# Layer 1's first two weights loaded during the feed-forward before it, and its preparations queued two blocks at a time

## The reference

```python
x = x + 0.5 * L0_ffn(layernorm(x))     # ternary weights, 8-bit activations, conv over time, silu
x = x + L0_attn(layernorm(x))          # softmax attention, 16 heads, bias b_o
x = x + 0.5 * L0_ffn(layernorm(x))
x = x + 0.5 * L1_ffn(layernorm(x))     # layer 1
x = x + L1_attn(layernorm(x))          # causal linear attention, strictly below the diagonal
x = x + 0.5 * L1_ffn(layernorm(x))
# L1_ffn:
p = softmax(x @ gate_W.T)                       # 8 experts
cnt[n, e] = number of experts of token n with p > 0.3, as a one-hot count
final = einsum over experts of (x @ expert_W[e].T) * cnt * p
return final @ out_W.T
```

## Time and profile before

| what | us |
|---|---|
| median of three runs | 3529.73 |
| the three runs | 3400.16, 3529.73, 3662.04 |
| the profiled execution | 3381.05 |
| span of its slowest core (3), first to last instruction | 3379.4 |
| spans of the other cores | 3299.0 to 3374.5 |
| TensorE busy, of the span | 2719.5 (80%) |
| VectorE busy | 1984.2 (59%) |
| ScalarE busy | 1703.0 (50%) |

### The profile page before, as it was taken

One profiled execution on the slowest core, in us unless ns is written; L12 is line 12 of the kernel. 1 busy time (PEld: TensorE's weight loads), 2 busy tenths in 40 slices (PEclk: granted clock), 3 DMA queues, 4 the chain that ended last, 5 costly groups with the idle time before them and its releaser, 6 DMA issues.

```text
span 3379.4 us, 39052 instructions; the slowest of 8 cores (3299.0 to 3379.4 us)
## 1 busy us (share of the span) xinstructions
PE 2719.5 (80%) x11770; PEld 1162.0 (34%) x11770; DVE 1984.2 (59%) x2842; ACT 1703.0 (50%) x2015; POOL 382.7 (11%) x437
## 2 busy tenths in 40 slices
PE   1355768799489999999999883678879959889789
PEld 0122223344133444444433331333334424334334
DVE  1477667775557777777765124677777514443433
ACT  2776656563423666666654623666656313414430
POOL 0000102112310001110000100001211211211310
PEclk7676889899798999999965796889989979999999
DMA  7343533233612022220110154122323360000001
GB/s 228 111 122 121 173 123 125 87 96 103 149 19 45 22 39 57 42 39 19 30 35 7 38 148 142 35 83 86 123 83 92 103 212 1 1 20 31 1 7 69
DMA packets 153945, 259.11 MB, mean 77 GB/s; under 512 B 37968, under 2 KB 74064, under 8 KB 153424
## 3 DMA queue, kind: packets, MB, share of 16 engines
q1 hardware_dynamic: 121312, 199.77, 19.4%
q0 software_dynamic: 32432, 56.83, 7.0%
HBM read 220.70 MB, written 52.56 MB: 81 GB/s over the span
## 4 chain that ended last, share of the span: by engine, by line
PE 61%; DVE 14%; ACT 9%; issue 8%; DMA 7%; POOL 1%; SPq 1%; DVEq 0%; ACTq 0%; POOLq 0%
PE fb L1099 11%; PE fb L869 8%; PE aups L1556 8%; PE apps L1670 7%; PE asps L1651 7%; PE mb L2169 6%; PE ajps L1520 3%; DVE fbig L910 2%; PE rs L2060 2%; DVE amx L1567 2%; ACT fbig L905 2%; PE mb L2224 2%; PE mb L1968 1%; DMA xbd<-alnb 1%; DMA fbig<-w1h 1%
## 5 line engine op out<-in xcount | busy, mean ns | idle before, releaser
L1567 DVE TENSOR_REDUCE amx<-aups 128x1 f32<-128x512 f32 x1024 | 662.6, 686 | 253.8 <-PE aups L1556 251.9
L1660 ACT ACTIVATE aet<-asps 128x1024 bf16<-128x1024 f32 x512 | 521.6, 1025 | 294.0 <-PE asps L1651 290.3
L869 PE MATMUL fb<-fxsc,fw1r 128*128 128x512 bf16 x2048 | 561.1, 415 | 96.4 <-DVE fbig L914 66.1
L1099 PE MATMUL fb<-fbig 128*128 128x512 bf16 x2048 | 504.1, 396 | 95.5 <-DVE fbig L839 53.8
L1556 PE MATMUL aups<-ahd 65*128 65x512 bf16 x1024 | 381.0, 415 | 22.1 <-DVE amx L1567 8.5
L1670 PE MATMUL apps<-aet,avt 128*65 128x512 bf16 x1024 | 339.8, 416 | 16.4 <-ACT aet L1660 11.0
L869 PEld LDWEIGHTS fb<-fxsc,fw1r 128*128 128x128 fp8e4 x2048 | 213.3, 105 | 400.6 <-issue 209.3
L1651 PE MATMUL asps<-ahd 65*128 65x512 bf16 x1024 | 340.0, 417 | 0.0
L1099 PEld LDWEIGHTS fb<-fbig 128*128 128x128 fp8e4 x2048 | 204.8, 101 | 362.2 <-issue 143.1
L910 DVE SCALAR_TENSOR_TENSOR fbig<-fb,cw2sb,fbig 128x511 f32<-128x511 f32 x256 | 191.3, 747 | 213.0 <-ACT fbig L905 210.8
L905 ACT ACTIVATE fbig<-fb,cbsb,cw2sb 128x512 f32<-128x512 f32 x256 | 196.3, 770 | 234.4 <-PE fb L869 222.0
(11 more groups left out here) (249 smaller groups left out, 2968.7 us busy)
## 6 DMA issues: line engine op xcount, KB each, us to landing
fw1r<-wq SPq DMA_DIRECT2D x224, 128.0 KB, 2.1
fbig<-wq SPq DMA_DIRECT2D x112, 256.0 KB, 2.7
fbig<-w1h SPq DMA_DIRECT2D x32, 512.0 KB, 12.9
fw2f<-w2h SPq DMA_DIRECT2D x64, 256.0 KB, 3.1
fbig<-w2h SPq DMA_DIRECT2D x28, 512.0 KB, 3.9
fxq<-x SPq DMA_DIRECT2D x8, 1024.0 KB, 9.0
fbig<-x POOLq DMA_DIRECT2D x32, 256.0 KB, 5.6
xa<-fbig POOLq DMA_DIRECT2D x32, 256.0 KB, 3.7
```

Source lines behind the costliest of these rows:

```text
L869: tp = T(lambda e, dc=dc: e.matmul(bank[b][:, :], sl[:, o + dc * 128:o + (dc + 1) * 128], xr[:, dc * 512:(dc + 1) * 512], start=(dc == 0), ...
L1099: tp = T(lambda e, j=j: e.matmul(bank[2 + j][:, :], w2r[s][:, o + j * 128:o + (j + 1) * 128], xi2[:, hc * 512:(hc + 1) * 512], start=(hc = ...
L1567: lambda e, hh=hh, c=c: e.tensor_reduce(m[:, c:c + 1], ups[hh][:, :], axis=AX.X, op=ALU.max),
L1660: ta = A(lambda e: e.activation(et[g % 3][:, :], sps[s][:, :], AF.Exp, scale=0.125), wait=[tp, tk.get(("ef", g % 3))])
```

## The change

Three shared places are made for the whole program: `sh_a` (16 KB a partition) serves as `xq` of the feed-forward, as `lnb` of the attention and as `qk` (so also `ow`) of layer 1; `sh_b` as `xsc`, `big2` and `xs[0]` (so also `e0`); `gw_sb` holds the gate weight, which is now loaded in the chain of constants at the head. `early_l1`, called at q = 4 of the second feed-forward, issues the loads of `owb` and `e0b` from SyncE as soon as the places are free, and `layer1` no longer issues them. In `center` POOL's subtraction of block k + 2 is emitted after the work on block k, and both preparations yield after the multiplications of blocks 1, 3 and 5, so that these go out in four pieces of two blocks. The function `attn_l0` is also moved up in the file, unchanged but for the two places.

```diff
+        gw_sb = sb("lgw", [128, DC * NE], F32)
+        sh_a = sb("sha", [128, DC * QT], F32)
+        sh_b = sb("shb", [128, 2 * DC * QT], BF16)
+        s_early = {k: em.sem("Se" + k) for k in ("ow", "e0")}
         s_pre = em.sem("Spre")
-        DMA_SEMS.append(s_pre)
+        DMA_SEMS += [s_pre] + list(s_early.values())
         pre = {}
...
         dma(CHX, cb_sb[:, :], cb_in.ap())
+        dma(CHX, gw_sb[:, :].rearrange("p (a m) -> p a m", a=DC),
+            gwT.ap().rearrange("(a p) m -> p a m", p=128))
         const_tag = dma(CHX, bo_sb[:, :], bo_in.ap())
...
                 em.wait_only(e, guard())
+        early = {}
+        def early_l1(w_a, w_b):
+            for key, dst, src, w in (("ow", sh_a[:, :].bitcast(BF16), owb,
+                                      w_a),
+                                     ("e0", sh_b[:, :], e0b, w_b)):
+                early[key] = em.go(
+                    "sync", lambda e, dst=dst, src=src: e.dma_start(
+                        dst.rearrange("p (a b) -> p a b", a=DC),
+                        src.ap().rearrange("(a p) m -> p a m", p=128)),
+                    wait=[pre[src.name]] + list(w), dma=s_early[key])
...
                 big = fsb("fbig", [128, 32 * 1024], F32)
-                xq = fsb("fxq", [128, DC * QT], F32)
+                xq = sh_a
                 xsb = fsb("fxs", [128, 2048], BF16)
...
                 xi8 = fsb("fxi8", [128, 2048], I8)
-                xsc = [fsb("fxsc", [128, DC * QT], BF16) for _ in range(2)]
+                xsc = [sh_b[:, i * DC * QT:(i + 1) * DC * QT]
+                       for i in range(2)]
                 acc = fsb("facc", [128, 1024], F32)
...
                     gen = first and q == 1
+                    if q == NQ and not first:
+                        early_l1([ln["xqfree"]], ln["xscfree"])
                     if q == 1:
...
                 wo = lsb("lwo", [128, KVC * D], BF16)
-                xs = [lsb("lxs", [128, 2 * DC * QT], BF16) for _ in range(2)]
+                xs = [sh_b, lsb("lxs", [128, 2 * DC * QT], BF16)]
                 xln = lsb("lxln", [128, DC * QT], BF16)
                 cb = [lsb("lc", [128, 512], F32) for _ in range(3)]
-                qk = lsb("lqk", [128, 4 * KVC * QT], BF16)
+                qk = sh_a[:, :].bitcast(BF16)
                 S_sb = lsb("ls", [128, KVC * KV], F32)
...
                 gt_sb = lsb("lgt", [8, 512], F32)
-                gw = lsb("lgw", [128, DC * NE], F32)
+                gw = gw_sb
                 gtok = lsb("lgk", [128, 128], F32)
...
                 s_o = dsem("lo")
-                s_g = dsem("lg")
...
-                tk["gw"] = dget(s_g, v3(gw[:, :], DC), gwT.ap().rearrange(
-                    "(a p) m -> p a m", p=128))
+                tk["ow"], tk["e0"] = early["ow"], early["e0"]
                 x_load(0)
-                w_load("ow", s_w[0], ow[:, :], owb, DC)
-                w_load("e0", s_w[1], xs[0][:, :], e0b, DC)
                 w_load("e1", s_w[2], xs[1][:, :], e1b, DC)
...
                         start=(dc == 0), stop=(dc == DC - 1)),
-                        wait=[tk["gw"]])
+                        wait=())
                 t = A(lambda e: e.mul(gtok[:, 0:NE], rs[0][:, 0:NE],
...
                 def center(q):
                     out = []
-                    for k in range(DC):
+                    def sub(k):
                         src = xq[q % 3][:, k * 512:(k + 1) * 512]
-                        t = G(lambda e, k=k, src=src: e.tensor_tensor(
+                        out.append(G(lambda e: e.tensor_tensor(
                             cb[k % 3][:, :], src, m_sb[:, :], ALU.subtract),
                             wait=[tk["m"], tk.get(("cf", k % 3)),
-                                  tk["x", q, k]])
-                        out.append(t)
-                        yield k, t
-                    tk["mf"] = t
+                                  tk["x", q, k]]))
+                    for k in range(2):
+                        sub(k)
+                    for k in range(DC):
+                        yield k, out[k]
+                        if k + 2 < DC:
+                            sub(k + 2)
+                    tk["mf"] = out[-1]
...
                         tk["cf", k % 3] = t
+                        if k % 2 == 1 and k < 7:
+                            yield
                     tk["rsf"] = [t]
...
                         tk["cf", k % 3] = t
+                        if k % 2 == 1 and k < 7:
+                            yield
                     tk["rsf"] = [t]
...
-                big2 = asb("abig2", [128, 4 * T], BF16)
+                big2 = sh_b
...
-                lnb = asb("alnb", [128, 4096], F32)
+                lnb = sh_a
```

947 lines of the change are left out of this document (472 added, 475 removed).

## The result

| | before | after |
|---|---|---|
| median of the runs of this comparison, us | 3464.94 (3394.69 to 3662.04) | 3489.99 (3348.45 to 3592.08) |
| ratio after / before, comparable runs | | 0.9863, 95% interval 0.9834 to 0.9891 |
| span of core 3 | 3379.4 | 3342.4 |
| core 3, layer 1 (start of the column means to the end of TensorE's last product) | 645.2 | 605.7 |
| core 3, TensorE busy | 2719.5 | 2715.6 |

In this comparison the changed kernel is about 1.4% faster, some 46 us of 3395. The medians say the opposite, because in some executions, the profiled one of the changed kernel among them, the cores of one die run at a lower clock and take up to 8% longer; the ratio leaves such executions out. Two later comparisons of the same two kernels gave 0.9883 (0.9841 to 0.9926) and 0.9915 (0.9893 to 0.9936), so about 1% is what all three bear out.

A forecast was written before the change was run, and what follows sets the result against it. TensorE's idle time in layer 1 was taken as the bound: the `e0b` wait and VectorE evictions. -16.2 - 0.9 + 2.6 - 23.8 = -38.3 us, off the median 3529.7 gives 3491; range 3339 to 3558.

The forecast's parts named there:

- The wait for `e0b`: Start of layer 1: TensorE's stand until `e0b` lands goes, so the fusion starts right after the column means, -16.2 us.
- second, third and fourth attention: Layer 1: preparations in pieces let evictions and output blocks come earlier, -3.8, -5.6 and -6.8 us.
- How the numbers follow: Closing step: 2% taken as tellable, sum taken off the median; faster 0.08, same 0.89, slower 0.03.
- Part 1, the two loads, w2's cover: Last feed-forward pass: early loads take 13.1 us, the w2 load queued behind keeps 6 us of cover, cost 0.
- Rival 4: Last feed-forward pass: the 4.19 MB hold back w2 loads; 14 us of wait at 112 GB/s; chance 0.04.
- The warmer clock: Start of the fusion: means running straight into it shorten its time at half clock, -0.9 us (0 to 1.75).
- The gate weight: Program's head: one more link in the chain of constants, +2.6 us; sign, first x load 2.4 to 3.9 later.
- The first attention: Layer 1: transposes end 5.1 us earlier, but the next normalisation's statistics slip three steps; -2.8 us.
- Rival 1: Layer 1 attentions: the statistics' slip takes the preparations' gain back to about 8 us, sum -22; chance 0.25.
- Rival 2: Layer 1: VectorE's order was the whole of the idle time, sum up to -78, middle -60 us; chance 0.13.
- Rival 3: Fusion start: early loads bring nothing because ScalarE's x casts delay TensorE; sum -21 us; chance 0.08.
- two signs that the prediction named for being wrong: Layer 1: TensorE waits longer for line 2350's evictions, or y blocks wait over 2 us a round for ScalarE's squares.

The follow-up runs named there:

- the preparations alone: Kernel before the change with only the two yields and the new `center`, weights still loaded in layer 1; ratio 0.9952 (0.9928 to 0.9976).
- the loads alone: Changed kernel with preparations in one piece and the old `center`; shared places, early loads and gate weight at the head kept; ratio 0.9973 (0.9948 to 0.9997).
- the last experiment: Changed kernel with statistics emitted beside the pieces, early loads behind the last w2 load, gate weight in layer 1; ratio to before 0.9843 (0.9827 to 0.986).

## Where the prediction was right, and the step that failed

**The sum.** -38.3 against -37.0 on the profiled core. The wait for `e0b`, the two normalisation places, second, third and fourth attention came within 0.3 us each. For the third attention some of that is luck: with the preparations alone the clock moved its length by over 2 us from core to core (76.1 against 73.5 to 73.7). That TensorE does not wait for the gate load in its 5 us behind SyncE's first issue held on core 3: 5.10 without the load, and 5.23 on seven cores when it was put back. It did not hold on every core: on core 6 of the kernel before it was the load that ended the wait, at 7.29. Three comparisons of the whole program (0.9863, 0.9883, 0.9915) lie around the forecast ratio of 0.9887.

**How the numbers follow** is the step that failed. "2% is about what a measurement of this kernel can tell from no change" stands there without a working; what it had at hand was the spread of three raw runs, 3400 to 3662. The runs showed a finer measure in its place: the ratio told 0.3% (0.9834 to 0.9891, and 0.2% to 0.4% in the repeats), and no change is outside all three intervals. A forecast of -1.1% should have been put as faster by a clear margin; the chance of 0.89 for no change, and 0.08 for faster, came from that one sentence. The second failing in the same paragraph is the base. Taking the sum off the median (3529.7) instead of off the profiled execution (3381.1 - 38.3 = 3343; the comparable runs of the changed kernel lay between 3338 and 3359) put the predicted time at 3491, a figure that depends on which of three widely spread runs is the middle one. The median of the changed kernel's four runs, 3490, fell next to it by chance; it is above the median of the kernel before, 3465, though the kernel is faster.

**Part 1, the two loads, w2's cover: wrong in size.** Forecast: issued at 2643, 13.1 us for both, first w2 load in by 2661, cover 6 us, cost 0. Measured: issued 2645.7 (SyncE was still issuing w2 loads to 2645.6), `e0b` landed 23.7 us later, at 2669.9, and the w2 product wanted at 2670.4 waited 0.37 us on core 3, 1.5 on core 2 and 3.9 on core 6. The w2 load that it waited for was issued at 2660.2 and took 10.4 us to land; in the kernel before the same load was issued at 2658.3, not 2656.5, and took 2.5. The term that was mis-sized is the rate: 321 GB/s was that of a stretch in which SyncE's queue moved 8.32 of the 8.34 MB. Here the engines moved

```profile
DMA packets 3323, 7.41 MB, mean 274 GB/s; under 512 B 224, under 2 KB 224, under 8 KB 3321
```

from 2645 to 2672, and only 4.19 of the 7.41 MB were the two weights; the rest were w2 weights, stores and residuals. Rival 4 named the place and the mechanism; its price was 0 to 4 us, and not 14 or more. The prediction cited the Trainium skill, "DMA: Bandwidth & Descriptors", Queues, rings and completion order, for the rule that a DMA engine consumes one ring's descriptors in order. The trace agrees with the rule: on core 3 the w2 load that was waited for came in at about 2670.6, behind `e0b` at 2669.9. The cost of 0 was worked out from a rate that wasn't there.

**The warmer clock.** Forecast -0.9 with bounds 0 and 1.75, measured -0.41 (fusion 72.17 us with the loads alone, 72.58 before). On the cores of the kernel before this length ran from 70.8 to 72.8, so the 0.41 is a difference of two slowest cores and no more. The clock reached its full level between 2741 and 2743, 4.1 us after the fusion's start and 7.5 after the means':

```profile
2739.00:2741.00 2.00, 2.00 (x6) 0.76 (x5) 0.00 (x0) 0.40 (x1) 0.00 (x0) 0.51 1.05 390
2741.00:2743.00 2.00, 2.00 (x10) 0.88 (x9) 0.38 (x1) 2.00 (x3) 0.00 (x0) 1.00 1.02 347
```

against 5.3 us after the fusion's start in the earlier trace rows. The means helped less than their 3.5 us.

**The gate weight.** Forecast +2.6, measured +2.87 for the link (18.06 to 20.93) and +2.6 at the start of the means. The first x load came at 22.54 on core 3 and had come at 20.55, 1.99 later, below the 2.4 to 3.9 that the prediction gave as its sign; over the eight cores the mean is 2.4 later. The Trainium skill, "DMA: Bandwidth & Descriptors", Anatomy of one DMA, gives a fixed cost of about 2.0 us, but it is fitted on transfers that GpSimd issues, and this load is SyncE's. The measurement decides: 2.2 to 3.5 us for the link on the cores of two executions, where the prediction had worked out 2.4 to 3.9 from its rows.

**The first attention.** Forecast -2.8, measured -1.2. By its own steps: the transposes ended 4.5 us earlier (forecast 5.1), but the third output block only 1.6 earlier (forecast 4.4), counted from the masks. The step that was wrong here is "ScalarE needs 2.4 us a round there (0.95 + 0.95 and an eviction of 0.5), TensorE 1.6, so the last statistics product ends at 2951.0": it took the y blocks at full clock. The granted clock was 1.00 to 0.98 until 2922; after the transposes' stand of 2.34 us it was 0.50 from 2922 to 2932:

```profile
2922.00:2926.00 4.00, 2.08 (x12) 1.28 (x12) 4.00 (x9) 3.01 (x5) 2.54 (x3) 0.50 0.00 0
2926.00:2932.00 6.00, 5.89 (x17) 2.29 (x18) 1.15 (x2) 4.92 (x7) 0.00 (x0) 0.50 0.00 0
```

so a round of y products and statistics took 2.8 us on TensorE (2927.77 to 2930.54), more than ScalarE's 2.4, and the reciprocal began 2.7 us later than forecast. The prediction had priced the half clock where a wait was to go, and not where one of 2 us was to stay.

**Rival 1** (the slip takes part 2 back) had 0.25. As a whole it is false: the preparations alone give 20 us. At the two places where it could act it is true of the first preparation's pieces, 4.6 and 1.9 us. **Rival 2** (all the standing was VectorE's order) had 0.13. Its amount did not come with this change, but emitting the second preparation's statistics earlier took 16 us more off layer 1 (55.7 in all, of which 16.4 are the wait for `e0b`); 60 was reached by no kernel here. **Rival 3** (the loads bring nothing) is refuted by the loads alone: the fusion starts 3.40 us after the means there too.

Neither of the two signs that the prediction named for being wrong came: the wait for line 2350's evictions (2380 now) went from 8.7 to 7.5 in total, and no round of y blocks waited more than 1.72 us for squares.

## What to carry to other kernels

Before a change is called too small to see, ask what the spread of the runs is made of: here 1% was told apart although the raw runs spread over 8%. When a block of work is cut into pieces between other work, list what is emitted behind it, and find out which wanted instruction the now later chain lands in front of: at two places a reciprocal that came three steps late left 6.6 of 24.4 us, and starting that chain in parallel with the pieces gave the rest. A prefetch that is issued early into a free place still shares the queue: issue it behind the loads that the running work wants next, and read more than one profile before a wait is called gone.

## What was not expected of the hardware

- 4.19 MB on SyncE's queue, beside POOL's stores and loads, took 21.3 to 27.4 us to land on the eight cores when issued at the head of the pass, and 15.0 to 20.9 us when issued behind the w2 loads; the rate that the load gets depends on what else the engines move (on core 3, 274 GB/s in all, 4.19 of 7.41 MB for it).
- After the same wait of 1.8 us, between the same products, the granted clock stayed at 1.00 in one kernel and fell to 0.50 for some 3.5 us in another (rows above; 2.4 and 1.2 GHz). The drop cost 1.8 us. It happens between the cores of one execution too: in the last experiment all eight cores had this wait of 1.8 us, and the fourth attention took 55.2 us on four of them and 53.8 on the other four (granted clock 0.50 from 3219 to 3221 on core 3, which is one of the slower four). Why it fell on the one and not on the other stays open; so a difference of 2 us between two profiles at such a place is no proof of an edit.
- TensorE began 5.1 us after SyncE's first issue behind the barrier on nearly every core without a load to wait for (4.6 to 4.9 on a few), and 5.1 to 5.2 with the gate load in front when that had landed in time. What it does in these 5 us the trace does not show; it was not tried apart.
